# Cross-attention scores from projected 64-dimension keys and queries, two heads at a time on two halves of the array's rows, under a fixed order of stages

## The reference, cut to what matters

```python
# x (4, 256, 128), context (4, 1601, 96), 8 heads of 64 dimensions
q = (layernorm(x) @ Wq).reshape(B, S, 8, 64)...
k = (context @ Wk).reshape(B, L, 8, 64)...
v = (context @ Wv).reshape(B, L, 8, 64)...
attn = softmax(einsum('bhsd,bhld->bhsl', q, k) / 8)
x = x + (attn @ v) @ Wo + bo
# then a layernorm and a mixture of 8 experts (128 -> 256 -> 128, top 2 of 8)
# beside a shared expert
x = x + shared(layernorm(x)) + mixed(layernorm(x))
```

## Time and profile before

| | |
|---|---|
| median of 3 runs | 431.85 us (431.66 to 433.05) |
| profiled execution | 430.69 us |
| its span | 428.6 us |
| first score product | 25.73 us |
| value products of pair 0, of pair 15 begin | 38.77 us, 361.48 us |
| PE, DVE, ACT, POOL busy | 98%, 65%, 51%, 60% |

### The profile page before, as it was taken

The page is one execution under the profiler, slowest core; times in us unless marked ns, Lnnn a source line. Parts: engine busy times, 40 slices in busy tenths (PEclk is TensorE's granted clock), DMA queues, the critical chain, the costliest instruction groups (busy, mean ns, idle before and its releaser), DMA issues.

```text
span 428.6 us, 7169 instructions
## 1 busy us (share of the span) xinstructions
PE 421.8 (98%) x2500; PEld 327.6 (76%) x2500; DVE 279.9 (65%) x556; ACT 218.2 (51%) x381; POOL 257.1 (60%) x174
## 2 busy tenths in 40 slices
PE   8999999999999999999999989999999999999997
PEld 7787777776887868777868777768777767778896
DVE  4786768786546859474348597754469597557653
ACT  3556253342663535335735242527624547689783
POOL 5518995878575749390756664463706460297981
PEclk9999999999999999999999998999999999999999
DMA  7400002000000020000000300000000011301500
GB/s 240 130 1 2 0 3 58 2 2 0 2 0 2 0 60 2 0 2 0 2 1 2 113 1 3 0 3 0 2 0 2 2 57 45 98 0 35 165 26 24
DMA packets 16329, 11.59 MB, mean 27 GB/s; under 512 B 9580, under 2 KB 13208, under 8 KB 16296
## 3 DMA queue, kind: packets, MB, share of 16 engines
q1 hardware_dynamic: 16296, 11.15, 9.5%
HBM read 10.55 MB, written 0.56 MB: 26 GB/s over the span
## 4 chain that ended last, share of the span: by engine, by line
PE 95%; DVE 2%; POOL 2%; ACT 1%; issue 1%; POOLq 0%
PE ps L1244 22%; PE ps L1164 12%; PE ps L1228 12%; PE ps L1229 11%; PE ps L1230 11%; PE ps L1076 8%; PE ps L1078 7%; PE ps L1077 7%; PE ps L1118 2%; PE ps L1176 1%; POOL g_lo L767 1%; PE ps L1084 1%; ACT ps L868 1%; DVE logit L1003 0%; PE ps L1094 0%
## 5 line engine op out<-in xcount | busy, mean ns | idle before, releaser
L842 ACT ACTIVATE probs<-ps 128x512 f32<-128x512 f32 (+1 forms) x208 | 123.8, 598 | 135.5 <-PE ps L1230 128.5
L969 DVE TENSOR_REDUCE maxes<-ps 128x1 f32<-128x402 f32 x256 | 131.8, 566 | 55.8 <-PE ps L1164 55.7
L562 POOL TENSOR_TENSOR work<-work,probs 128x1024 f32<-128x1024 f32 x54 | 128.9, 2387 | 19.5 <-ACT probs L842 16.8
L1244 PE MATMUL ps<-probs,v_sb 128*64 128x256 f32 (+1 forms) x832 | 93.4, 381 | 0.0
L560 POOL TENSOR_TENSOR work<-probs 128x1024 f32<-128x1024 f32 x14 | 33.5, 2390 | 86.2 <-issue 60.6
L1244 PEld LDWEIGHTS ps<-probs,v_sb 128*64 128x64 f32 (+1 forms) x832 | 58.4, 137 | 33.9 <-ACT probs L842 3.3
L1228 PE MATMUL ps<-g_hi,ctxT_hi 97*128 97x512 f32 (+1 forms) x208 | 83.4, 401 | 0.0
L1229 PE MATMUL ps<-g_lo,ctxT_hi 96*128 96x512 f32 (+1 forms) x208 | 82.5, 397 | 0.0
L1230 PE MATMUL ps<-g_hi,ctxT_lo 96*128 96x512 f32 (+1 forms) x208 | 82.1, 395 | 0.0
L1164 PE MATMUL ps<-ctxT_hi,g_hi 96*128 96x402 f32 x256 | 73.6, 359 | 2.0 <-DVE maxes L969 1.9
L1164 PEld LDWEIGHTS ps<-ctxT_hi,g_hi 96*128 96x128 f32 x256 | 46.9, 190 | 17.8 <-DVE maxes L969 5.1
(11 more groups left out here) (145 smaller groups left out, 524.6 us busy)
## 6 DMA issues: line engine op xcount, KB each, us to landing
v_sb<-weight_rows SPq DMA_DIRECT2D x12, 256.0 KB, 4.2
raw<-in_ctx_T_dram SPq DMA_DIRECT2D x3, 600.4 KB, 4.7
work<-in_L_ffn_rw_dram SPq DMA_DIRECT2D x1, 1024.0 KB, 7.0
raw<-weight_rows SPq DMA_DIRECT2D x4, 256.0 KB, 3.5
g_hi<-neg_row SPq DMA_DIRECT2D x60, 0.5 KB, 2.0
raw<-in_ctx_T_dram SPq DMA_DIRECT2D x3, 150.8 KB, 3.0
x_sb<-in_x_dram SPq DMA_DIRECT2D x1, 384.0 KB, 4.9
early<-in_WqkT_dram SPq DMA_DIRECT2D x1, 336.0 KB, 4.4
```

The lines of the kernel that those rows point to most:

```text
L562: ops.tensor_tensor(acc, acc, pr, ALU.add).then_inc(summed, 1)
L842: nc.scalar.activation(probs[0:rows, n % SLOTS, j, :], s_bank(chunk_no(*w))[0:rows, :], ACT.Exp, scale=SCALE).then_inc(probs_ready, 1)
L969: v.tensor_reduce(maxes[:, p % 2, i * T + t, blk:blk + 1], src[:, 0:BW], AX.X, ALU.max).then_inc(ring_taken, 1)
L1244: ins = mm(o_bank[DH * i:DH * (i + 1), :], v_sb[0:rows, c, h * DH:(h + 1) * DH], probs[0:rows, n % SLOTS, j, i * S:(i + 1) * S], start=(c ...
```

## The change

What it does:

- Keys and queries are projected: for each pair `("k", b, p, block)` makes four blocks of 402 keys (three products each) and `("q", b, p)` the 256 queries (three products). ACT copies the high part, DVE subtracts for the low part. Weights are split at the start; `product_of_weights` and "g" go.
- A chunk's scores are eight products of 64 rows by 256 columns: four factors (high by high, high by low, low by high, and ones by the shift), each for head 0 on rows 0 to 63 and head 1 on rows 64 to 127, into two PSUM banks.
- A maximum has 64 rows too, and the two heads of one tile and block stand side by side.
- Scores of a unit take two banks, two units take four; the ring keeps three (4, 5, 6). The exponent is taken a unit at a time (1024 wide).
- `plan` is a fixed list. In a pair: seven units, with two maxima of the next pair behind each of the first five; then the projections for the pair after the next (with the values' projections of the batch); then three maxima of that pair, the 26 value products, the sums, and three more maxima.
- DVE adds probabilities in the last pair only, and POOL up to pair 14.

```diff
+    for n, (b, p) in enumerate(order):
+        ahead = maxima[n + 1][2 * EARLY_MAXIMA:] if n + 1 < n_order else []
+        behind = 2 if n == 1 else 0
+        for u in range(n_units):
+            out.append(("scores", (b, p, u)))
+            out += ahead[:2]
+            if ahead and len(ahead) <= 2:
+                out.append(("shift", order[n + 1]))
+            ahead = ahead[2:]
...
+            if n and u in (behind, behind + 1):
+                out.append(("quotient", order[n - 1] + (u - behind,)))
...
+        projections = keys(n + 2)
+        if vs:
+            for i, x in enumerate(projections or vs[:1]):
+                out += ([x] if projections else []) + vs[2 * i:2 * i + 2]
+            out += vs[2 * len(projections or vs[:1]):]
+        else:
+            out += projections
...
+        if n == 1:
+            out += [("normal", t) for t in range(1, batches)] + [("ring", ("xn", 0)), ("ring", ("xn", 1))]
...
+        out += following[:EARLY_MAXIMA]
+        out += [("values", (b, p, u, j)) for u, unit in enumerate(key_units(chunks)) for j in range(len(unit))]
...
+        out += [("sums", (b, p))] * (0 < n < n_order - 1)
+        out += following[EARLY_MAXIMA:2 * EARLY_MAXIMA]
```

```diff
-            bank = min(range(O_BANK - (RING if wide else 2 if late else 3), O_BANK), key=lambda i: held.get(i, -1))
+            lowest = 2 if n < kinds.index("scores") else 4 if n < kinds.index("first") else 5
+            bank = min(range(lowest, O_BANK), key=lambda i: held.get(i, -1))
...
-            return "dve" if u == NU - 1 or pair >= B * PAIRS - 2 or pair == B * PAIRS - 3 and u >= 4 else "pool"
+            return "dve" if pair and u == NU - 1 or pair == B * PAIRS - 1 else "pool"
...
+                elif kind == "ring" and w[0] in ("k", "q"):
+                    act.wait_ge(ring_filled, ring_no[w] + 1)
+                    hi, _, src = key_parts(w)
+                    nc.scalar.copy(hi, src).then_inc(kq_hi_ready, 1)
...
+                    src, dst = score_banks(n), probs[:, n % SLOTS]
...
+                    nc.scalar.activation(dst, src, ACT.Exp, scale=SCALE).then_inc(probs_ready, 1)
...
+                    elif w[0] in ("k", "q"):
+                        dve.wait_ge(kq_hi_ready, hi_no[w] + 1)
+                        hi, lo, src = key_parts(w)
+                        v.tensor_tensor(lo, src, hi.bitcast(F32), ALU.subtract).then_inc(ring_taken, 1)
...
-                        ins = mm(dst[:, 0:BW], g_hi[0:C, b % 2, 2 * p + i, t * P:(t + 1) * P],
-                                 ctxT_hi[0:C, b % 2, k0:k0 + BW], start=True, stop=True)
+                        ins = mm(dst[:, 0:BW], q_hi[rows, pair % 4, t * P:(t + 1) * P],
+                                 k_hi[rows, pair % 2, k0:k0 + BW], start=True, stop=True)
...
-                    mm(dst, ctxT_hi[:, b % 2, ks], gh, start=True, stop=False)
-                    mm(dst, ctxT_hi[0:C, b % 2, ks], gl, start=False, stop=False)
-                    ins = mm(dst, ctxT_lo[:, b % 2, ks], gh[0:C], start=False, stop=True)
+                    if n >= 2:
+                        pe.wait_ge(probs_ready, n - 1)
+                    banks = score_banks(n)
+                    for j, c in enumerate(UNITS[u]):
...
+                        factors = ((hi, q_hi[:, pair % 4, :]), (hi, q_lo[:, pair % 4, :]), (lo, q_hi[:, pair % 4, :]),
+                                   (ones_r[:, 0:rows], shift_rows[:, p % 2, :]))
+                        for i, (keys, queries) in enumerate(factors):
+                            for h in range(2):
+                                dims = slice(DH * h, DH * h + DH)
+                                ins = mm(banks[0:rows, h, j * S:(j + 1) * S], keys[dims], queries[dims],
+                                         start=(i == 0), stop=(i == len(factors) - 1))
```

More of the change, by code:

```diff
@@ L42, in key_units @@
     return [list(range(c, min(c + 2, chunks))) for c in range(0, chunks, 2)]
[L46 to L50, removed]
@@ L53, in plan @@
 def plan(batches, pairs, chunks, heads_per_pair, tiles, blocks, halves, experts):
-    units = key_units(chunks)
-    n_units = len(units)
+    n_units = len(key_units(chunks))
     order = [(b, p) for b in range(batches) for p in range(pairs)]
-    tasks = [("g", 0, 0)]
-    n_v0 = 0
-    for n, (b, p) in enumerate(order):
-        maxima = [("max", b, p, i, t, k) for i in range(heads_per_pair) for t in range(tiles)
-                  for k in range(blocks)]
-        put = {}
-        if n == 1:
[L66 to L104, removed]
@@ new lines, in plan, with keys @@
+    n_order = len(order)
+    maxima = [[("ring", ("max", b, p, i, t, k)) for k in range(blocks) for t in range(tiles)
+               for i in range(heads_per_pair)] for b, p in order]
+    couples = [maxima[0][i:i + heads_per_pair] for i in range(0, len(maxima[0]), heads_per_pair)]
+    def keys(n):
+        if n >= n_order:
+            return []
+        b, p = order[n]
+        return [("ring", ("k", b, p, 0)), ("ring", ("q", b, p))] + [("ring", ("k", b, p, k)) for k in range(1, blocks)]
+    first, second = keys(0), keys(1)
@@ new lines, in plan @@
+    v0 = [("v0", c) for c in range(chunks)]
+    out = first[:2] + [("ctx0", 2)] + first[2:3] + [("ctx0", 3)] + couples[0] + couples[1] + first[3:4]
+    out += [("wv", 0)] + couples[2] + couples[3] + first[4:] + [("m", 0)]
+    for i, pair_of_maxima in enumerate(couples[4:]):
+        out += pair_of_maxima + v0[i:i + 1]
+    out.append(("shift", order[0]))
+    rest = v0[len(couples) - 4:]
+    out += rest[:2]
+    for i, x in enumerate(second):
+        out += [x] + rest[2 + i:3 + i]
+    out += rest[2 + len(second):] + maxima[1][:2 * EARLY_MAXIMA]
@@ L295, in build @@
     kinds = [kind for kind, _ in steps]
-    amid = range(kinds.index("scores"), len(kinds) - kinds[::-1].index("values"))
     ring_banks, ring_last, held = [], [], {}
@@ L517, in activations, with key_parts @@
             return hid[:, n % 4, :] if items[n][1] == E else hid_w[:, n % 8, :]
-        def m_parts(i):
-            bank, n = ((0, 1), (2, PAIRS - 1))[i]
-            hi, lo = (m.rearrange("p (a two) c -> p two a c", two=2)[:, :, i:i + n, :] for m in (m_hi, m_lo))
-            return hi, lo, ps[:, bank:bank + 2, 0:n * C].rearrange("p two (a c) -> p two a c", a=n)
+        def key_parts(w):
+            pair, k = w[1] * PAIRS + w[2], ring_no[w]
+            if w[0] == "q":
+                return q_hi[:, pair % 4, :], q_lo[:, pair % 4, :], ring(k)[:, 0:S]
+            cs = quarter(w[3])
+            first = cs.start - min(cs.start, L - BW)
+            return k_hi[:, pair % 2, cs], k_lo[:, pair % 2, cs], ring(k)[:, first:first + cs.stop - cs.start]
         block = ctx.enter_context(nc.Block())
```

408 lines of the change are left out of this document (147 added, 261 removed).

## The result

The changed kernel takes 470.45 us (median of 4 runs, 468.46 to 473.51), the kernel before 431.77 us in the same session: a ratio of 1.0895, 95% interval 1.0824 to 1.0966. The profiled execution took 468.46 us, its span is 466.6 us, 38.0 more than before. The forecast was 452.0, range 432 to 476.

What follows compares the result with a forecast made beforehand. PE, busy 98% of the span, was taken as the bound. The pairs' periods add 17.8 us and the start 2.5 to the span of 428.6, giving 448.9; 2.1 around it and 1.2 for the median make 452, range 432 to 476.

Steps and rivals of the forecast that it cites:

- Two halves side by side: PE's scores: two 64-row products, one on each half, load and run together, a couple in 0.118 us.
- the sum by loads in a line: Rival for PE's scores: the halves do not overlap, a couple costs 0.222 us, 508 us in all; chance 0.06.
- DVE's quotients hold the ring: Scores' stage: maxima wait for banks behind DVE's two quotients; PE stands 3.5 to 4.3 and 5.6 to 6.5 us.
- The pair: A plain pair from values to values: 21.1 us, 17.1 of PE's work and 3.9 of waits, against 20.3 measured before.
- my sum of 19.3: PE's own work per pair in the kernel before: products, maxima, "g", values and sums 19.0 us, with two tiling changes 19.3.
- Behind the last pair: The end, from the last values' start: the experts stand as before, 67.1 us.
- Mis-sized: the start: Up to pair 0's scores: first score product at 28.3 us (+2.6), first values at 41.3 (+2.5).
- that cover: Time between DVE's last addition and a plain pair's sums, 3 us; if gone, PE would wait at the sums.
- The readings that I named: Signs in the profile: PE busy near 85%, waiting some 30 us for DVE's maxima and some 20 for k's low parts.
- DVE keeps up: Rival: maxima behind a quotient do not hold the scores, 2.3 us of waits go in 14 pairs, 420 us; chance 0.17.
- my layout: The step-by-step sum of work and waits over start, pairs and end: 452 us, band 436 to 464, chance 0.56.
- the clock rival: PE's clock falls in the new waits, some 1.5 us in each of 14 pairs, 473 us (464 to 478); chance 0.17.

Runs made afterwards that it cites:

- e2: The changed kernel with DVE's two quotients of a pair moved from behind units 0 and 1 (2 and 3 in pair 1) to behind units 5 and 6; 471.3 us.
- e8: The changed kernel with the head's loop outermost in a unit, eight score products of head 0, then eight of head 1; 491.07 us.
- e5: The changed kernel with more empty products around the transposes of x and 20 more between pair 0's projections and maxima; 461.74 us.
- e10: The changed kernel with e5's start, e9's quotients, e4's maxima, pair 1's transposes behind its values, and pair 14's unit-5 addition on DVE; 439.34 us.
- e11: e10 with the first of pair 14's additions (units 0 and 1) on DVE in place of the fifth (unit 5); 437.02 us.
- e4: The changed kernel with the three early maxima between projections and values moved into the values, behind their fourth unit; 452.43 us.
- e3: The changed kernel with the scores' loops over head and factor exchanged, four products of head 0, then four of head 1; 473.06 us.
- e6: The changed kernel with 12 empty products (4 and 8) in the projections' stage of each pair without value projections; 473.87 us.
- e9: The changed kernel with the quotients behind the unit-3 and unit-4 maxima, in the last pair where they stood before; 459.95 us.

## Why the prediction was right, and where it was off

- **Two halves side by side**: 0.118 a couple predicted, 0.12 measured. The sentence of the Trainium skill that a load takes as long as its columns (TensorE: Matmul & The Clock Gate, "LDWEIGHTS") holds here in that the rows do not matter: a load's record of 128 columns lasts 0.19 with 64 rows and with 128, one of 64 columns 0.14. But two loads on two halves overlap, so the sum by loads in a line, 508 us, did not come (its terms, 11.5 - 6.1 - 2.3 = 3.1 a pair and not 3.5, give 502):

```profile
L1126 PEld LDWEIGHTS ps<-kq_hi,kq_lo 64*128 64x128 f32 x384 | 62.8, 186 | 0.0
...
L1141 PEld LDWEIGHTS ps<-probs,v_sb 128*64 128x64 f32 x768 | 55.9, 143 | 31.5 <-issue 7.7
...
L996 PEld LDWEIGHTS ps<-kq_lo,w_hi 128*128 128x128 f32 x54 | 10.2, 189 | 0.9
```

- **DVE's quotients hold the ring**: predicted waits that end 4.3 and 6.5 us into the stage and last 0.8 and 0.9, measured 4.4 and 6.6 (88.13 and 90.29 from 83.70) with 0.74 and 0.93; stage 9.4 predicted, 9.52 measured, and e2 takes 1.8 of it away. "PSUM Bottleneck" of the Trainium skill's TensorEngine Tiling (Array Packing), tiling speeds up PE and not what empties PSUM, is borne out by e8: 2.8 us more of PE's work in a stage made it 0.6 longer.
- **The pair**: 21.1 predicted, 21.32 measured (pair 3, away from the falls). For the kernel before, my sum of 19.3 fits pair 7, 19.25; the 20.30 of pair 3 that I set beside it holds 1.0 us more, so that the plain pair lost up to 2.1. Scores to values 14.4, measured 14.82. With value projections 29.1 and 29.67; "y" 22.2 and 22.35; router 21.6 and 21.58; pair 14 17.1 and 17.02; pair 1 26.0 and 24.97; exponent 1.0, measured 1.03:

```profile
L772 ACT ACTIVATE probs<-ps 128x1024 f32<-128x1024 f32 x96 | 98.1, 1026 | 148.4 <-PE ps L1126 145.0
```

- **Behind the last pair** 67.1, measured 466.6 - 399.52 = 67.1.
- **Mis-sized: the start.** 28.3 predicted, 36.48 measured. e5 parts the 8.2: 5.9 were the clock, 2.3 the rest, most likely the hand-over of k and q, longer than laid out (e5's empty products may be in it). Pair 0 adds 0.9 up to its values, and that makes 9.1 of the 17.7 us by which the span was missed.
- **Mis-sized: the clock in the pairs.** I gave a fall in each pair a chance of 0.17 and took none into the sum; three falls came (pairs 1, 3, 6), some 5 us. That the clock falls once PE waits was right, the place not: the largest part lay at the start, which I had not looked at for waits.
- **Mis-sized: pair 15**, 14.8 predicted, 16.22 measured: pair 14's sums came 2.1 late. I had given that cover 3 us for a plain pair, and forgot that pair 14 has no projections to add to it, and that the change hands pair 14's additions from DVE to POOL. The remaining 2.3 of the pairs' 8.7 are 0.2 to 0.6 in each pair but 1, 11 and 14, less the 1.0 of pair 1.
- **The readings that I named**: PE's waits for maxima 15.4, not 30, and PE busy 92%, not 85%. The two waits of a stage cost what was laid out; the list is shorter, as shown at 89.24, and products at half the clock count as busy. The 2.3 that I took for all waits of the stage were too much: e2 got back 1.8, and about 7.5 is the floor that the exponents set.
- **The rival "DVE keeps up"** did not come, by the place of the quotients and of the early maxima: with both moved, e10 and e11 reach 18.9 for a plain pair, close to its number. And still the change does not pay. I had put the saving in PE's own work at 2.2 a pair; e11's fifteen periods save 0.8 in all. By the records PE idles 15.1 us between the values of pairs 0 and 15 in e11, 30.8 in the change and 1.6 before, 7.9 of e11's for the low part of k. How much of the rest the added changes of tiling take (0.17 each in e4) no run measures.
- **The number itself**: 470.45 lies in the range, but not in the 436 to 464 that I gave my layout. It lies in the band of the clock rival (464 to 478, chance 0.17), and near its 473 by chance, since that was fourteen falls in the pairs and not a start at one half. Without the 5.9 us of the start and the 5 of the pairs the change would stand near 460, inside my layout's band. The order of the kernels and the waits for DVE were foreseen; the size was met by the width of the range.

## What to carry to other kernels

Before taking work from the busiest engine, lay out what the next one does in the same stage: where its queue has no gap, saved products come back as waits, and moving its work a few places can just move the wait, as e2 did. Then lay out the engine after that: here the exponents would have been next. Lay out the start as carefully as the steady part, and count a chain that goes hand over hand between engines there as a risk to TensorE's clock. Take the cost of a wait from the distance of two starts, not from the list of waits. Take the duration of an instruction from rows of one shape: the page's mean of the exponents, 962 ns, mixes 96 of 1024 columns at 1026 with 16 of 512. And look at several executions before you call a fall of the clock the effect of an edit.

## What the runs showed of the hardware that was not expected

- After two waits within 3 us (0.78 and 0.97) PE's clock stood at one half for 20.5 us, although PE was busy 20.2 of them by its records; with the same start but a second wait of at most 0.39 in e2, e3, e4, e6, e8 and e9 the clock fell between 12.8 and 14.3 us and stood at one half for 10.2 to 13.7 us.
- Products on two halves of the array's rows run together even when four of one half are written ahead of four of the other (stage 9.54 for 9.52), and no longer fully with eight and eight (10.11). They start out of their written order: at 89.20 a maximum starts ahead of a score product that is written before it, at 89.24.
- An exponent over two PSUM banks, 1024 wide, takes 1.03 us where two of 512 take 1.20.
